# VectorE's order in a recurrent layer: taps, softplus parts, gate and low products placed between instructions that depend on each other

## The reference

```python
xc = conv_b
for j in range(K):                                  # K = 4 taps
    xc = xc + conv_w[:, j] * xpad[:, j:j + L, :]
x = silu(xc)
...
dt = softplus(ts @ W_dt.T + b_dt)
def step(state, inp):                               # 1024 steps, 1024 channels x 16 states
    dA = exp(dt_t[..., None] * A)
    state = state * dA + (dt_t * u_t)[..., None] * B_t[:, None, :]
    y = einsum('bdn,bn->bd', state, C_t)
y = (ys + x * D) * silu(gate)
return y @ W_out.T
```

## Time and profile before

| | |
|---|---|
| median of three runs | 1072.48 us |
| profiled execution | 1074.76 us, span 1072.9 us |
| VectorE busy | 996.6 us, 93% of the span, 1025 instructions |
| GpSimd busy | 909.7 us, 85% |
| TensorE busy | 861.6 us, 80%, granted clock 0.906 in the mean |
| ScalarE busy | 727.6 us, 68% |

### The profile page before, as it was taken

One profiled execution on the slowest core, in us unless ns is written; L12 is line 12 of the kernel. 1 busy time (PEld: TensorE's weight loads), 2 busy tenths in 40 slices (PEclk: granted clock), 3 DMA queues, 4 the chain that ended last, 5 costly groups with the idle time before them and its releaser, 6 DMA issues.

```text
span 1072.9 us, 10234 instructions
## 1 busy us (share of the span) xinstructions
PE 861.6 (80%) x2756; PEld 319.1 (30%) x2756; DVE 996.6 (93%) x1025; ACT 727.6 (68%) x1281; POOL 909.7 (85%) x322
## 2 busy tenths in 40 slices
PE   8943557988978998898846859889897999679568
PEld 5321112333323333333211313333332343223122
DVE  6779988999999989999999899999999989999997
ACT  3657656788787766788565566688777666567543
POOL 0617898997989998888798979799988988999996
PEclk9976668999999999999876879999998999889779
DMA  9847668767778576666743752965648556664725
GB/s 336 345 158 285 223 235 330 278 247 267 263 266 333 183 270 241 228 257 212 259 113 143 217 194 109 320 231 191 228 149 303 217 215 235 216 220 182 274 42 154
DMA packets 86585, 245.93 MB, mean 229 GB/s; under 512 B 9344, under 2 KB 10752, under 8 KB 79872
## 3 DMA queue, kind: packets, MB, share of 16 engines
q1 hardware_dynamic: 67712, 197.03, 51.4%
q10 hardware_dynamic: 12672, 31.46, 7.4%
q0 software_dynamic: 6144, 16.78, 5.8%
HBM read 183.11 MB, written 62.13 MB: 229 GB/s over the span
## 4 chain that ended last, share of the span: by engine, by line
DVE 30%; PE 22%; POOL 21%; issue 11%; DMA 9%; ACT 5%; SPq 2%; DVEq 0%; ACTq 0%; POOLq 0%
DVE sc_ps L1175 13%; POOL drive L588 12%; DVE drive L1175 8%; PE x_ps L1458 5%; POOL drive L601 4%; PE f_ps L1411 4%; DMA rep<-rep_rows 4%; PE y_ps L1426 3%; PE dt_ps L1386 2%; DMA rep_rows<-dtu 2%; DVE x_ps L1114 2%; DVE drive L1185 2%; PE x_ps L1322 2%; POOL moe L573 2%; ACT sc_ps L801 1%
## 5 line engine op out<-in xcount | busy, mean ns | idle before, releaser
L588 POOL TENSOR_TENSOR drive<-rep,b_all 128x2048 f32<-128x2048 f32 x127 | 578.9, 4598 | 46.6 <-DMA rep<-rep_rows 40.5
L801 ACT ACTIVATE sc_ps<-rep,a_neg 128x512 f32<-128x512 f32 x512 | 332.0, 681 | 93.3 <-DVE drive L1185 63.4
L601 POOL TENSOR_TENSOR drive<-drive,c_all 128x1024 f32<-128x1024 f32 x94 | 224.2, 2385 | 20.6 <-ACT state L780 12.8
L1426 PE MATMUL y_ps<-drive,stack 128*32 128x512 f32 x1024 | 153.5, 675 | 107.1 <-POOL drive L601 59.8
L1175 DVE TENSOR_TENSOR_SCAN sc_ps<-sc_ps,state,drive 128x512 f32<-128x512 f32 x164 | 201.0, 1272 | 4.7 <-ACT sc_ps L801 2.4
L1185 DVE TENSOR_TENSOR drive<-sc_ps,c_all 128x1024 f32<-128x1024 f32 x162 | 198.4, 1224 | 5.4
L1175 DVE TENSOR_TENSOR_SCAN sc_ps<-sc_ps,drive 128x512 f32<-128x512 f32 x160 | 186.5, 1211 | 14.6 <-ACT sc_ps L801 7.4
L1411 PE MATMUL f_ps<-w_ring,xT_slot 128*128 128x512 f32 x368 | 171.8, 611 | 14.9 <-ACT xT_slot L811 14.7
L1386 PE MATMUL dt_ps<-xnT,w_g 128*128 128x512 f32 x232 | 126.8, 697 | 27.5 <-ACT dtu L768 27.5
L1175 DVE TENSOR_TENSOR_SCAN drive<-sc_ps,state,drive 128x512 f32<-128x512 f32 x92 | 112.7, 1266 | 3.4 <-ACT sc_ps L801 3.4
L1175 DVE TENSOR_TENSOR_SCAN drive<-sc_ps,drive 128x512 f32<-128x512 f32 x96 | 111.7, 1205 | 0.0
(11 more groups left out here) (187 smaller groups left out, 1034.0 us busy)
## 6 DMA issues: line engine op xcount, KB each, us to landing
rep<-rep_rows SPq DMA_DIRECT2D x128, 512.0 KB
w_ring<-wring SPq DMA_DIRECT2D x46, 1024.0 KB, 5.4
rep_rows<-dtu ACTq DMA_DIRECT2D x32, 512.0 KB
x_slot<-slot_x SPq DMA_DIRECT2D x46, 256.0 KB, 7.0
slot_rows<-y_slot ACTq DMA_DIRECT2D x46, 256.0 KB
w_g<-wg_in SPq DMA_DIRECT2D x32, 256.0 KB
w_x<-wx_in SPq DMA_DIRECT2D x24, 256.0 KB
slot_x<-zeros SPq DMA_DIRECT2D x1, 5888.0 KB, 20.5
```

Source lines behind the costliest of these rows:

```text
L588: pool.tensor_tensor(drive[:, m % RING, :, :], rep[:, n % 2, :, 1, :], b_all[:, q:q + 1, :].broadcast_to([P, NR, TC]), ALU.mult).then_inc( ...
L601: pool.tensor_tensor(drive[:, m % RING, 0:2, :], drive[:, m % RING, 0:2, :], c_all[:, q:q + 1, :].broadcast_to([P, 2, TC]), ALU.mult).then ...
L801: act.activation(sc[:, r, :], rep[:, n % 2, r, 0, :], ACT.Exp, scale=a_neg[:, lo:lo + 1]).then_inc(decay_ok, 1)
L1426: last = pe.matmul(y_ps[CH * r:CH * (r + 1), :], stack[:, :], drive[:, m % RING, r, :], start=False, stop=(m % NQ == NQ - 1))
```

## The change

Only VectorE's order changes, with two new semaphores. `convolve` is cut into `tap(j, k)`, `step_sizes` into `larger_part`, `less_rounding`, `plus_log` and `times_x`, `scans` into `scan(m, r)` of one row. In the loop over tiles:

- the low product (where VectorE makes it) stands behind the scan of row 2, no longer ahead of it, in every quad;
- the early taps stand behind the scans of rows 0, 1 and 2 of the second quad;
- in late tiles the first scan of the fourth quad is moved ahead of the high product of the third, and the late taps stand behind that product and the scans of rows 1 and 2;
- in the 12 tiles of `STEPS_AMONG_SCANS` the softplus of tile n+2 starts ahead of the fourth quad's last scan and ends behind the first scan of the next tile;
- in the tiles not in `GATE_BEHIND` the gate stands ahead of the first quad's high product.

The instructions are the same 1025. The core of the diff (the definitions of `tap`, `larger_part`, `less_rounding`, `plus_log` and `scan` hold the same operations as before):

```diff
+STEPS_AMONG_SCANS = (1, 3, 5, 10, 15, 16, 17, 19, 21, 26, 27, 29)
+GATE_BEHIND = (3, 5, 9, 10, 15, 18, 19, 21, 25, 26, 27, 29, 30)
...
+            def tap(j, k):
                 c, t = divmod(j, NT)
-                dve.wait_ge(tap_ok, j + 1)
+                if k == 1:
+                    dve.wait_ge(tap_ok, j + 1)
+                else:
+                    dve.wait_ge(tap_sum, 2 * j + k - 1)
...
-                    low(m)
+                    scan(m, 0)
+                    if n - 1 in STEPS_AMONG_SCANS:
+                        times_x(n + 1)
+                    scan(m, 1)
                     if pe_log(n + 1):
                         times_x(n + 1)
-                    scans(m, 1)
+                    scan(m, 2)
+                    low_product(m)
+                    scan(m, 3)
                     if chunk_end and not pe_log(n + 1):
                         step_sizes(n + 1)
+                    if n not in GATE_BEHIND:
+                        gate_tile(n - 1)
                     products(m, 1)
-                if n:
-                    gate_tile(n - 1)
-                low(m + 1)
+                    if n in GATE_BEHIND:
+                        gate_tile(n - 1)
+
+                scan(m + 1, 0)
                 if early is not None:
-                    convolve(NT * (c + 1) + early)
-                scans(m + 1, 1)
+                    tap(NT * (c + 1) + early, 1)
+                scan(m + 1, 1)
+                if early is not None:
+                    tap(NT * (c + 1) + early, 2)
+                scan(m + 1, 2)
+                low_product(m + 1)
+                if early is not None:
+                    tap(NT * (c + 1) + early, 3)
+                scan(m + 1, 3)
                 if after_odd and t == 2:
                     out_tile(c - 1, 3)
                 products(m + 1, 1)
-                low(m + 2)
+
+                scan(m + 2, 0)
+                scan(m + 2, 1)
                 if after_odd and t == 1:
                     out_tile(c - 1, 0)
-                high(m + 2)
+                scan(m + 2, 2)
+                low_product(m + 2)
+                scan(m + 2, 3)
                 if late is not None:
-                    convolve(NT * (c + 1) + late)
+                    scan(m + 3, 0)
                 if after_odd and t == 1:
                     out_tile(c - 1, 1)
-                low(m + 3)
-                high(m + 3)
-                if rms_tile:
+                products(m + 2, 1)
+
+                if late is not None:
+                    tap(NT * (c + 1) + late, 1)
+                else:
+                    scan(m + 3, 0)
+                scan(m + 3, 1)
+                if late is not None:
+                    tap(NT * (c + 1) + late, 2)
+                scan(m + 3, 2)
+                low_product(m + 3)
+                if late is not None:
+                    tap(NT * (c + 1) + late, 3)
+                if n in STEPS_AMONG_SCANS:
+                    larger_part(n + 2)
+                scan(m + 3, 3)
+                if n in STEPS_AMONG_SCANS:
+                    less_rounding(n + 2)
+                products(m + 3, 1)
+                if n in STEPS_AMONG_SCANS:
+                    plus_log(n + 2)
+                elif rms_tile:
                     rms(c + 1)
```

More of the change, by code:

```diff
@@ L274, in scan_moe @@
         pad_ok, tap_ok, halo_ok = sem("pad_ok"), sem("tap_ok"), sem("halo_ok")
+        tap_sum, part_ok = sem("tap_sum"), sem("part_ok")
         conv_ok, x_ok = sem("conv_ok"), sem("x_ok")
@@ L1103, in route_weights, with convolve @@
                 dve.tensor_tensor(p2[:, :], e2, r1, ALU.mult).then_inc(prob_ok, 1)
-            def convolve(j):
+            def tap(j, k):
                 c, t = divmod(j, NT)
-                dve.wait_ge(tap_ok, j + 1)
-                if c == 1:
+                if k == 1:
+                    dve.wait_ge(tap_ok, j + 1)
+                else:
+                    dve.wait_ge(tap_sum, 2 * j + k - 1)
+                if k == K - 1 and c == 1:
                     dve.wait_ge(s_stage, 16 * (NCH - 2))
                     dve.wait_ge(lgT_mm, 1)
-                if c >= 2:
+                if k == K - 1 and c >= 2:
                     dve.wait_ge(o_mm, TT * (c - 1))
+                dve.scalar_tensor_tensor(out=x_bank(j) if k < K - 1 else xy[:, c % 2, t, :], in0=padded(j)[:, k:k + TC],
+                                         scalar=cw[:, t * K + k:t * K + k + 1], in1=x_bank(j),
+                                         op0=ALU.mult, op1=ALU.add).then_inc(tap_sum if k < K - 1 else conv_ok, 1)
+            def convolve(j):
                 for k in range(1, K):
[L1114 to L1120, removed]
+                    tap(j, k)
             spreads(1)
@@ L1150, in times_x, with larger_part, less_rounding, plus_log @@
                 dve.tensor_tensor(u, dt_ps[:, :], xy[:, c % 2, t, :], ALU.mult).then_inc(dt_ok, 1)
-            def step_sizes(k):
[L1153 to L1158, removed]
+            def larger_part(k):
+                dve.wait_ge(ln_ok, k + 1)
+                dve.scalar_tensor_tensor(out=dt_ps[:, :], in0=dt_ps[:, :], scalar=0.0, in1=t_e[:, :],
+                                         op0=ALU.max, op1=ALU.add).then_inc(part_ok, 1)
+            def less_rounding(k):
+                dve.wait_ge(part_ok, 2 * (k - pe_logs(k)) + 1)
+                dve.scalar_tensor_tensor(out=dt_ps[:, :], in0=t_w[:, :], scalar=-1.0, in1=dt_ps[:, :],
+                                         op0=ALU.add, op1=ALU.subtract).then_inc(part_ok, 1)
+            def plus_log(k):
+                dve.wait_ge(part_ok, 2 * (k - pe_logs(k)) + 2)
+                dve.tensor_tensor(dt_ps[:, :], t_l[:, :], dt_ps[:, :], ALU.subtract).then_inc(sp_ok, 1)
+            def step_sizes(k):
+                larger_part(k)
+                less_rounding(k)
+                plus_log(k)
                 times_x(k)
-            def scans(m, h):
+            def scan(m, r):
                 n, q = divmod(m, NQ)
                 c, t = divmod(n, NT)
-                if m == 0 and h == 0:
+                if m == 0 and r == 0:
                     dve.wait_ge(first_half, 1)
-                elif m == 0 or h == 0:
+                elif m == 0 or r == 0:
                     drives_done(dve, m + 1)
@@ L1169, in scans @@
                 if follows:
[L1170 to L1177, removed]
+                    dve.wait_ge(state_ok, kept_states(m - NQ * NT) + r // 2 + 1)
+                lo = column(t, q, r)
+                to = drive[:, m % RING, r, :] if r < 2 and on_pool(m) else sc[:, r, :]
+                dve.wait_ge(decay_ok, NR * m + r + 1)
+                dve.tensor_tensor_scan(to, sc[:, r, :], drive[:, m % RING, r, :],
+                                       state[:, lo:lo + 1] if follows else 0.0,
+                                       ALU.mult, ALU.add).then_inc(scan_ok, 1)
             def products(m, h):
@@ L1187, in products, with low_product @@
                                   ALU.mult).then_inc(high_ok if h else low_ok, 1)
-            def low(m):
-                scans(m, 0)
+            def low_product(m):
                 if not on_pool(m):
                     products(m, 0)
-            def high(m):
-                scans(m, 1)
-                products(m, 1)
             def gate_tile(n):
@@ L1232, in _ @@
             route_rows()
-            for h in range(2):
-                scans(0, h)
-                products(0, h)
+            scan(0, 0)
+            scan(0, 1)
+            low_product(0)
+            scan(0, 2)
+            scan(0, 3)
+            products(0, 1)
             route_weights()
```

1 line of the change is left out of this document (removed).

## The result

The changed kernel takes 1080.04 us (median of 5 runs, 1078.03 to 1080.39); before, run beside it, 1071.75 (5 runs, 1070.03 to 1073.99). The ratio is 1.0066, 95% interval 1.0052 to 1.0080: 0.66% slower, 7.1 us of 1072.5 (5.6 to 8.6 by the interval; the two medians lie 8.3 us apart). The forecast was +3.6 us, slower; so the sign is right, and the size is half of what was measured, with 1080 inside the range (1060 to 1083). The profiled execution of after took 1079.08 us with a span of 1077.3 us; that of before had 1072.9 us.

The account below looks back on a forecast made before the run. VectorE's own sequence was taken to bound most tiles, shared with GpSimd in the last. Spacing -12.6, late tiles +10.3 and low products +5.9 gave +3.6 us: 1072.48 to 1076, range 1060 to 1083.

Parts of the forecast that it names:

- The spacing: VectorE: 158 fewer instructions wait for the one just before them, 0.118 us each; 107 count, 12.6 us gained.
- The late tiles: VectorE waits for ScalarE's decay at the fourth quad's moved first scan in late tiles: 10.3 us lost.
- the upper bound: Waits at the fourth quad's first scan in late tiles: at most 16 us, if nothing is deducted.
- The low products: Second quad's later low product releases ScalarE later; VectorE waits at the third quad's row 2: 5.9 us lost.
- the upper bound on half of the late waits: Fourth quad's first scan in late tiles: upper bound 16 us applied to half the waits, named as giving 1083.
- the upper bound on the low products: Waits behind VectorE's later low products: at most 10 us, against 5.9 forecast.
- ScalarE is in time: Rival, 0.28: no waits at the fourth quad's first scan in late tiles; faster, 1066, or 1060 without low-product waits.
- Spacing gives nothing: Rival, 0.04: VectorE's 0.09 us overlap comes from instruction kinds; the 12.6 us gain falls away, waits stay: 1087.
- The new waits replace old ones: Rival, 0.17: VectorE's waits elsewhere shorten, taking back a third of 16.2 us; no change, 1071 to 1072.5.

Follow-up runs that it names:

- the added waits: "Both" with early taps and two late ones also waiting for the scan just ahead, 59 places more: 1071.32 us, ratio to before 0.9986.
- Both: After, with late tiles' fourth-quad first scan back behind high product and one tap, and low products ahead of row 2's scan: 1063.81 us, ratio to before 0.9921.
- late front scan undone: After, with the fourth quad's first scan in late tiles back behind the high product and one tap: 1068.69 us, ratio to before 0.9962.

## Why the prediction was right, and where its size was off

- **The spacing, 12.6 us.** The price stands (0.118 by the added waits, the taps' starts, busy time 14.6 us less). The share that reaches the end is bracketed only. "Both" is 0.79% faster, 8.5 us for 120 places; the other 38 of after are worth at most 4.5 us more: 8.5 to 13. Where it arrives is not shown: 48 softplus places gave 5.3 us, 59 taps 7.0 (5.7 for the 48 that the change had freed) and 16 gates nothing. That is 11 us for a whole of 8.5, each uncertain by about 2.
- **The late tiles, 10.3 us.** The mechanism and the places hold, and most sizes: 1.05 for 1.0 in tile 4, 2.97 for 2.9 in tile 10, 2.02 for 2.2 in tile 19. The size that failed is that of tiles 5 and 21: they wait 2.0 us each, where I had 1.2. The waits sum to the 16 us of the upper bound, and three pairs of kernels put what reaches the end at 10 to 12.5 us.
- **The low products, 5.9 us.** Tiles 17 and 31 came as worked out, 2.15 and 2.32 for 2.3, and tile 14 has 0.91 for 1.25. Moving them back gives 5.6 us, or 4.4 ("late front scan undone" against "both"), net of 26 places that return, so they cost 4.4 to 8.7.
- **The step that failed** is in this term: I followed each low product to ScalarE, and took it that nothing else is behind it. Behind the last one stands TensorE's output product of the last tile, and the end of the kernel hangs on it. By the traces 2.7 us were missing there. Whether tiles 24 to 30, 6 and 22 add a little each can't be told from these runs.
- **The sum.** With these 2.7 us the forecast would have been +6.3, inside the measured 5.6 to 8.6; what is left is less than the runs can tell. The sum is not shown term by term: the two re-orderings together cost 15.5 us and up to 4.5 more (16.2 stood there), and the spacing gave 8.5 to 13, and only their difference is firm.
- **Luck in the stretches.** After starts tile 3 at 179.4, tile 10 at 388.4, tile 17 at 611.9, tile 24 at 826.1 and tile 31 at 1031.0 us. Against before that is -0.9 us up to tile 3 (forecast 0), then +3.3 up to tile 10 (forecast -0.4), -3.2 up to tile 17 (-0.2), +1.6 up to tile 24 (+2.3) and +3.6 to the end (+1.7). The two large errors cancel. Of the +3.3, 2.8 us are the softplus wait of tile 8 (3.40 for 0.59), which the kernel with only the last low product moved, of the same order up to tile 31, does not have (0.81).
- **The range.** Its upper end does not follow from the working it names: the upper bound on half of the late waits adds 2.9 us and gives 1079, under the measured 1080.04. 1083 needs the upper bound on the low products (4.1 us) as well.
- **The rivals.** "ScalarE is in time" needed a lag below 9.3 us in tile 4; it stayed at 10.23. "Spacing gives nothing" fell with the added waits. "The new waits replace old ones" held only where the prediction had counted it, as for TensorE in tile 19 (2.11 us at 683.22 before, 0.36 after): taking back the two re-orderings gave at least 15.5 us, nearly the whole 16.2.

## What to carry to other kernels

To put something between dependent steps of an engine is worth measuring (here 0.12 us a place, 0.8% in all, and 1.0% with the copy moved), as long as what is put there does not pull an instruction ahead of data that another engine makes. Before moving an in-order instruction up, take the release-to-ready time of its producer from the trace and compare it with the work left on the consumer in between; if that work is shorter, look for something on the producer's side that can go behind, as the copy here. When an instruction is moved down, follow its result to every engine that uses it, and at the very end of the kernel too, where nothing takes up a delay.

## What was not expected of the hardware

What a short idle time at the end costs TensorE through its clock is almost as much as the idle time itself. After 2.10 and 2.15 us without work in two kernels the next 8 matmuls took 5.37 us. In the eight kernels where the trace has no such gap ahead of them they took 3.70 us, and after 0.32 us in another 3.67. In after the granted clock was 0.50 for 3.4 us of them, from half a us behind the idle time on. So a wait of 2.1 us made 3.8 on TensorE, of which 2.7 reached the end of the kernel.
